# Reading a matmul's moving columns from last to first in a two-layer attention and feed-forward kernel

## The reference, cut to what matters

```python
x = x + L0_xattn(layernorm(x), ctx, ctx, mask, wq, wk, wv, wo)      # 32 query heads, 8 key heads of 128, with rotary positions
x = x + L0_ffn(layernorm(x), w_gate, w_up, w_down)                  # inner width 1376, integer-valued
x = x + L1_xattn(layernorm(x), ctx, Wq, Wk, Wv, Wo, q_norm_w, k_norm_w)  # keys from ctx and x, RMS norms
x = x + L1_ffn(layernorm(x), gamma, beta, w1, b1, w3, b3)           # two int8-like 512x512 layers
```

## Time and profile before

| | |
|---|---|
| median of 3 runs | 1535.55 us (1535.22 to 1535.87) |
| profiled execution, first to last instruction (its span) | 1536.3 us |
| TensorE matmuls busy | 1481.3 us, 96% of the span |
| TensorE weight loads busy | 1273.9 us (they overlap the matmuls) |
| VectorE busy | 950.8 us |
| ScalarE busy | 599.3 us |
| GpSimd busy | 564.6 us |
| mean granted TensorE clock | 0.989 of 2.4 GHz |

### The profile page before, as it was taken

One profiled execution on the slowest core, in us unless ns is written; L12 is line 12 of the kernel. 1 busy time (PEld: TensorE's weight loads), 2 busy tenths in 40 slices (PEclk: granted clock), 3 DMA queues, 4 the chain that ended last, 5 costly groups with the idle time before them and its releaser, 6 DMA issues.

```text
span 1536.3 us, 28681 instructions
## 1 busy us (share of the span) xinstructions
PE 1481.3 (96%) x11533; PEld 1273.9 (83%) x11536; DVE 950.8 (62%) x1983; ACT 599.3 (39%) x1434; POOL 564.6 (37%) x468
## 2 busy tenths in 40 slices
PE   6899999999999998999899999999999999999985
PEld 5788888888888877887788899888889989888973
DVE  7656666665666575666866455555645645565588
ACT  4313222221222234442355354444435444443556
POOL 4535354443535414561233132222312222231248
PEclk9999999999999999999899999999999999999999
DMA  6101021111102003220112011011101111010201
GB/s 197 42 28 53 19 68 29 42 38 33 48 22 70 21 6 98 75 57 21 48 30 62 1 42 29 28 43 28 42 1 42 29 29 42 21 50 1 83 2 55
DMA packets 84302, 64.45 MB, mean 42 GB/s; under 512 B 7280, under 2 KB 71024, under 8 KB 84176
## 3 DMA queue, kind: packets, MB, share of 16 engines
q1 hardware_dynamic: 83600, 62.47, 14.1%
q10 hardware_dynamic: 576, 0.20, 0.1%
HBM read 60.56 MB, written 2.10 MB: 41 GB/s over the span
## 4 chain that ended last, share of the span: by engine, by line
PE 47%; DVE 2%; POOL 1%; issue 1%; ACT 0%; DVEq 0%; ACTq 0%; POOLq 0%
PE att_proj L70 35%; PE att_att L798 4%; PE att_sco L756 4%; PE att_att L773 2%; PE att_proj L720 1%; PE att_sco L735 1%; POOL ffn_y L476 0%; DVE ffn_top L428 0%; DVE ffn_y L470 0%; POOL x_rows L414 0%; DVE ffn_y L424 0%; PE att_att L242 0%; DVE stats L383 0%; DVE x_rows L1051 0%; ACT ffn_y L435 0%
## 5 line engine op out<-in xcount | busy, mean ns | idle before, releaser
L148 POOL TENSOR_TENSOR att_w_lo<-w_raw,att_w_hi 128x512 fp32r<-128x512 f32 x160 | 207.0, 1319 | 183.3 <-ACT att_w_hi L143 175.8
L1414 POOL TENSOR_TENSOR att_probs<-att_probs,att_total 128x512 f32<-128x512 f32 x64 | 82.9, 1295 | 458.5 <-DVE att_total L1035 344.5
L70 PE MATMUL att_proj<-att_w_hi,kv_hi 128*128 128x256 f32 x768 | 221.7, 289 | 9.7 <-DVE kv_lo L260 9.7
L70 PE MATMUL att_proj<-att_w_hi,kv_lo 128*128 128x256 f32 x768 | 216.5, 282 | 0.0
L70 PE MATMUL att_proj<-att_w_lo,kv_hi 128*128 128x256 f32 x768 | 216.4, 282 | 0.0
L70 PE MATMUL att_proj<-kv_hi,att_w_hi 128*128 128x512 f32 x512 | 208.7, 408 | 1.5 <-DVE kv_lo L251 1.5
L70 PE MATMUL att_proj<-att_w_hi,att_o_hi 128*128 128x512 f32 x512 | 207.0, 404 | 1.9 <-issue 1.9
L70 PE MATMUL att_proj<-kv_lo,att_w_hi 128*128 128x512 f32 x512 | 202.7, 396 | 0.0
L70 PE MATMUL att_proj<-kv_hi,att_w_lo 128*128 128x512 f32 x512 | 202.6, 396 | 0.0
L70 PE MATMUL att_proj<-att_w_lo,att_o_hi 128*128 128x512 f32 x512 | 201.5, 394 | 0.0
L1051 DVE TENSOR_TENSOR x_rows<-att_proj,x_rows 128x512 f32<-128x512 f32 x128 | 88.4, 691 | 182.4 <-PE att_proj L70 182.3
(11 more groups left out here) (167 smaller groups left out, 2743.6 us busy)
## 6 DMA issues: line engine op xcount, KB each, us to landing
w_raw<-in_wq SPq DMA_DIRECT2D x64, 256.0 KB, 2.9
w_raw<-in_wo SPq DMA_DIRECT2D x64, 256.0 KB, 2.8
w_raw<-in_wk SPq DMA_DIRECT2D x16, 256.0 KB, 3.0
w_raw<-in_wv SPq DMA_DIRECT2D x16, 256.0 KB, 3.5
w_raw<-in_gate_t SPq DMA_DIRECT2D x10, 256.0 KB, 2.9
w_raw<-in_up_t SPq DMA_DIRECT2D x10, 256.0 KB, 3.2
w_raw<-in_down_t SPq DMA_DIRECT2D x10, 256.0 KB, 3.0
spare<-in_ctx_t SPq DMA_DIRECT2D x4, 512.0 KB, 5.2
```

The source lines that it names most:

```text
L70: ins = eng.matmul(out, a, b, start=(first and n == 0), stop=(last and n == 3 * len(terms) - 1))
L148: eng.tensor_tensor(self.lo[:, chunk], self.raw[:, n % RAW_SLOTS], raw(self.hi[:, chunk]), ALU.subtract)\
L1414: eng.tensor_tensor(probs[:, u % 2, 0:n], probs[:, u % 2, 0:n], total[:, u % 2, 0:n].unsqueeze(2).broadcast_to([P, n, KL]), ALU.mult)\
```

## The change

A helper `backward` reverses the free dimensions of an access pattern. The split products pass their output and their moving operand through it, and so does the down projection. The first column that enters the array is then the last one of the operand, and it is written to the last column of the output, so that every result stands where it stood. The stationary operands are as before.

```diff
+def backward(ap):
+
+    return ap[:, ::-1] if len(ap.shape) == 2 else ap[:, ::-1, ::-1]
+
 def split_product(eng, out, terms, first=True, last=True):
     n = 0
     for lhs_hi, lhs_lo, rhs_hi, rhs_lo in terms:
         for a, b in ((lhs_hi, rhs_hi), (lhs_lo, rhs_hi), (lhs_hi, rhs_lo)):
-            ins = eng.matmul(out, a, b, start=(first and n == 0), stop=(last and n == 3 * len(terms) - 1))
+            ins = eng.matmul(backward(out), a, backward(b), start=(first and n == 0),
+                             stop=(last and n == 3 * len(terms) - 1))
             n += 1
     return ins
...
-                        last = eng.matmul(out_bank(t)[:], hid[:m, c, t * P:(t + 1) * P], down[:m, c, :],
+                        last = eng.matmul(backward(out_bank(t)[:]), hid[:m, c, t * P:(t + 1) * P], backward(down[:m, c, :]),
                                           start=(c == 0 and i == 0), stop=(c == CF - 1 and i == 1))
```

## The result

| | before | after |
|---|---|---|
| median of 4 runs each, us | 1535.71 (1535.22 to 1536.12) | 1550.47 (1549.44 to 1551.05) |
| span of the profiled execution, us | 1536.3 | 1549.3 |
| mean granted TensorE clock | 0.989 | 0.990 |

The changed kernel is slower: the ratio is 1.0095, interval 1.0083 to 1.0107, or 15 us. All lines of the code lie 4 or 5 further down: line 70 is now 74, line 1774 is 1779.

A forecast was written before the change was run, and what follows sets the result against it. The prediction took TensorE's matmuls, busy 1481.3 of 1536.3 us, to bound the kernel. Adding 0 ns for each of 6080 matmuls left a 1536.3 us span, 1535.5 us on the runs' scale; range 1500 to 1565 us.

The forecast's parts named there:

- What bounds the kernel: Whole kernel: TensorE's matmuls, busy 1481.3 of 1536.3 us, set the time; VectorE would need over 500 us more first.
- The counts and the present steps: Line 70 and line 1774: 3776 matmuls of 512 columns at 230 ns and 2304 of 256 at 118 ns.
- I take 230 ns: Step assumed for every 512-column matmul, from 226.6 ns in the first attention and 233.3 ns in the second.
- 0 ns for each of the 6080: Line 70 and line 1774: reading and writing backward adds no time to any changed matmul.
- the jumps of the queries: Second attention: query products read 8 runs of 64 columns with gaps, at 233.6 ns against 233.2 for the output projection.
- seven jumps cost 0.4 ns at most: Second attention: bound on the gaps between the query products' 8 runs, from 233.6 against 233.2 ns.
- The write: Changed matmuls: writing output columns backward costs nothing; VectorE and ScalarE see them at the same moment.
- The small-loss rival: First attention and feed-forward stage go to 233.3 ns: 2240 x 6.7 ns = 15 us, 1551 us; chance 0.14.
- turns with the weight load: Changed matmuls: the weight load beside each takes turns at the memory, so direction could move the step either way.
- Half rate: All changed matmuls take their half-clock steps, 427 and 213 ns: 963 us more, about 2490 us; chance 0.20, including partial loss.
- Its 8 us for matmuls already at half clock: Part of the 963 us loss not due, because some changed matmuls already run at half clock (mean clock 0.989).
- Small gain: Changed matmuls fall toward the bf16 step: at most 57 and 24 us, 1455 us; likely 1516 us; chance 0.12.

The follow-up runs named there:

- all tiles at 32: Kernel before, all forward, plus unused pads putting the second attention's moving and stationary tiles at byte 32 modulo 128: 1534.03 us, ratio 0.9983.
- the zigzag: Kernel before, but gate and up read moving columns backward inside ascending pieces of 16, output forward: 1556.13 us, beside 1536.91 for the kernel before.

## Why the prediction was wrong

*What bounds the kernel* was right. TensorE's busy time grew by 12.8 us and the span by 13.0, no other engine hid any of it, and no wait was new.

*The counts and the present steps* were right, but "I take 230 ns" averaged over two levels, 226.7 and 233.3 ns, and of the 512-column steps only those at the lower one lost much.

*The step that failed* is the one in which "a backward walk stays in the same lines of memory, each used as often as before" became "0 ns for each of the 6080". The first half is true and the kernel turned round inside 16 bytes shows that it is free. It leaves out the order of the lines. From the jumps of the queries I argued that "addresses that don't simply count up are no trouble as such". Those runs are 64 columns long and go upward inside, and the kernel with reversed pieces of 64 shows the same, 227.3 ns. Below 64 columns the matter changes, and no row that I used had shorter runs. Further, I had tested that claim in the second attention, where the step was already at the backward level: a stage that hides the loss. With all tiles at 32 the same 8 runs cost 4 ns more than the output projection beside them (232.4 against 228.4), so "seven jumps cost 0.4 ns at most" holds for the tiles' places in the kernel before, not for jumps as such. In place of the 0 ns the runs showed up to 5.7 ns for a matmul of the first attention, 6.2 in gate and up, 4.4 in down, next to nothing for 512 columns in the second attention and, for 256 columns, 2.3 more there and 1.3 less in the first.

*The write* at nothing was right: ratio 1.0001.

*The small-loss rival* came about at its price. It said that first attention and feed-forward stage go to 233.3 ns, 2240 x 6.7 ns = 15 us, 1551 us; measured were 1550.47. By stage the agreement is looser, by the table of steps. Gate and up lost 3.3 us where 528 x 6.7 = 3.5 was due, down 0.8 where 1.2 was. The first attention lost 6.4 us where 1536 x 6.7 = 10.3 was due: its queries stood at 229.5 ns before, not at 226.7, and its keys and values got faster. The second attention, for which the rival had nothing, lost 3.9 us, nearly all in its 1536 matmuls of 256 columns, a shape that the rival left out. Its total was thus right partly by luck: two misses of about 4 us cancel. Its stated cause, turns with the weight load, isn't supported: halving the load or reading it from one address left the backward step of 512 columns at 233.3 ns.

*Half rate* didn't occur: no step at full clock came near 427 or 213 ns. (Its 8 us for matmuls already at half clock were rough: a mean of 0.989 leaves 34 us at half clock, so up to 16 us.) *Small gain* didn't either, though a gain of 0.23% was there to be had by moving tiles.

*The range* of 1500 to 1565 us held the time. The chance of 0.14 for the case that happened was too small: two levels for one shape, in rows I had read, said that something like reading order or place could move the step by just these 6.7 ns, and where it stood at the lower one, upward.

**Open.** Why the backward step is 233.3 ns and the zigzag 266.5, what between 16 and 64 columns makes the difference, why bf16 is free, why the places of the two tiles count forward, and why 256 columns go their own way (backward 118.4 ns in the first attention and 119.9 in the second). That two reads collide in the memory would fit, but no run shows it. The pieces of 64 bytes began 32 bytes past a multiple of 64, since the moving tile of gate and up stands at 32 modulo 128; whether their numbers depend on that wasn't tried. Nor were reversing the stationary operand and matmuls without a weight load beside them.

## What to carry to other kernels

Let the moving operand of fp32 matmuls be read upward in runs of at least 64 columns (4 and 16 lost, 64 and 256 didn't; nothing between was run). The output's direction, and the order inside 16 bytes, were free here. Where TensorE bounds the kernel, look at the steps between starts in each stage: two levels for one shape are a hint that something may be gained, here by the tiles' places modulo 128 bytes (0.23%, with 512 columns gaining and 256 losing). And test "this costs nothing" on a stage that stands at the lower level, since one at the upper level may not show the loss. Compare stages by their steps at an equal granted clock, not by their lengths.

## What the runs showed of the hardware that I had not expected

- The same 512-column fp32 matmul at a granted clock of 1.00 has steps of 226.7, 233.3 or 266.5 ns, by the order of reading and the tiles' places; in bf16 215 ns in either direction.
- Moving and stationary tile at the same place modulo 128 bytes suit 512 columns in one run (226.7 ns) and not 256 (119.7); 64 bytes apart it is 233 and 117.6.
- The backward step of 512 columns is more even than the forward one: 233.3 to 233.9 ns in all stages, whatever the weight load reads; only one placement gave 235.0, in the queries with 8 runs.
- Unused tiles of 96, 96 and 32 bytes made the kernel 0.23% faster (0.13 to 0.33).
